# Attention and a routed feed-forward layer on one core: every engine's instruction order laid out anew, and six repeated products per batch removed

## The reference

```python
x = x + xattn(layernorm(x), ctx, ctx)      # x is (16, 128, 256), ctx (16, 128, 64)
x = x + ffn(layernorm(x), gate_w, w1, w2, w3)

# xattn: 32 query heads of 8 columns share 8 key/value heads
scores = einsum('bkgsd,bktd->bkgst', qh, kh) / sqrt(8)
out = einsum('bkgst,bktd->bkgsd', softmax(scores), vh)

# ffn: 8 experts, two chosen for each of the 2048 rows
probs = softmax(x @ gate_w.T)
weights, chosen = top_k(probs, 2);  weights = weights / weights.sum()
y = sum over the chosen e of weights[e] * (silu(x @ w1[e].T) * (x @ w3[e].T)) @ w2[e].T
```

## Time and profile before

| | |
|---|---|
| median of 3 runs | 457.79 us (457.29 to 458.43) |
| the profiled execution, its own time | 456.95 us |
| its span, first to last instruction | 455.1 us |
| busy: PE, DVE, ACT, POOL | 360.5, 236.6, 194.9, 196.3 us |
| mean granted TensorE clock | 0.933 of full speed |

### The profile page before, as it was taken

How to read it: one execution, slowest core, us unless ns; L and a number is a source line. 1 busy time by engine, 2 the same in 40 slices (tenths; PEclk the granted TensorE clock), 3 DMA queues, 4 the chain that set the end, 5 groups by cost and what they waited for, 6 DMA issues and landing times.

```text
span 455.1 us, 8617 instructions
## 1 busy us (share of the span) xinstructions
PE 360.5 (79%) x2255; PEld 256.4 (56%) x2256; DVE 236.6 (52%) x649; ACT 194.9 (43%) x397; POOL 196.3 (43%) x371
## 2 busy tenths in 40 slices
PE   0168789897988798752108999999999999999991
PEld 0044445454444354322107888888888888888871
DVE  6768777878777576638682322333222332223220
ACT  3325678675776465966303223222232222322220
POOL 6651355478564645575740223222233222332222
PEclk9999999999999898975557999999999999999997
DMA  6675877887988871320421332332333333223221
GB/s 191 163 146 108 254 217 217 202 237 192 256 230 246 200 219 65 120 81 23 163 81 35 49 59 46 49 56 46 58 47 47 56 47 58 46 47 57 36 23 23
DMA packets 46209, 51.16 MB, mean 112 GB/s; under 512 B 18659, under 2 KB 39267, under 8 KB 46179
## 3 DMA queue, kind: packets, MB, share of 16 engines
q1 hardware_dynamic: 37299, 39.64, 33.1%
q0 software_dynamic: 7152, 9.34, 13.1%
q10 hardware_dynamic: 1728, 1.82, 1.3%
HBM read 31.51 MB, written 16.69 MB: 106 GB/s over the span
## 4 chain that ended last, share of the span: by engine, by line
PE 53%; POOL 9%; issue 7%; DVE 5%; DMA 4%; ACT 3%; SPq 1%; POOLq 1%; ACTq 0%; DVEq 0%
PE bank L872 24%; PE bank L890 15%; PE bank L882 4%; DMA qst<-negT 3%; PE bank L704 2%; PE bank L860 2%; POOL slots_d L529 2%; PE bank L717 2%; PE bank L681 2%; ACT prob L941 1%; POOL x L500 1%; PE bank L678 1%; POOL rs L548 1%; DMA slots_d<-rows,slot 1%; DVE tx L1444 1%
## 5 line engine op out<-in xcount | busy, mean ns | idle before, releaser
L644 POOL DMA_INDIRECT out_rows<-ys,meta x39 | 60.6, 1554 | 153.0 <-DVE ys L1480 142.7
L1215 DVE TENSOR_REDUCE negm<-bank 128x4 f32<-128x512 f32 x128 | 83.2, 679 | 23.9 <-PE bank L681 23.3
L941 ACT ACTIVATE prob<-bank 128x512 f32<-128x512 f32 x128 | 73.6, 595 | 29.4 <-PE bank L704 28.0
L1473 DVE TENSOR_TENSOR gat<-bank,sil 128x512 f32<-128x512 f32 x39 | 27.0, 692 | 112.5 <-PE bank L872 112.5
L890 PE MATMUL bank<-w,gT 128*128 x312 | 73.9, 380 | 0.8 <-ACT gT L1135 0.8
L1129 ACT ACTIVATE sil<-bank 128x512 f32<-128x512 f32 x39 | 23.3, 597 | 105.9 <-PE bank L872 105.9
L704 PE MATMUL bank<-qst,kst 128*128 128x512 bf16 x128 | 49.6, 393 | 19.6 <-DMA qst<-negT 16.7
L872 PE MATMUL bank<-whi,xhi 128*128 x156 | 60.3, 468 | 1.2 <-ACT xhi L1123 1.2
L890 PEld LDWEIGHTS bank<-w,gT 128*128 128x128 f32 x312 | 56.3, 190 | 7.1 <-issue 1.0
L681 PEld LDWEIGHTS bank<-kst,qst 125*128 125x128 bf16 x512 | 41.4, 102 | 21.2 <-issue 3.1
L681 PE MATMUL bank<-kst,qst 125*128 125x128 bf16 x512 | 51.8, 227 | 0.0
(11 more groups left out here) (121 smaller groups left out, 493.7 us busy)
## 6 DMA issues: line engine op xcount, KB each, us to landing
xs<-slots_d SPq DMA_DIRECT2D x39, 129.0 KB, 2.1
w<-in_w1T SPq DMA_DIRECT2D x8, 512.0 KB, 4.6
w<-in_w3T SPq DMA_DIRECT2D x8, 512.0 KB, 4.6
w<-in_w2T SPq DMA_DIRECT2D x8, 512.0 KB
qparts_d<-qp SPq DMA_DIRECT2D x16, 192.0 KB, 5.4
qst<-qparts_d SPq DMA_DIRECT2D x16, 192.0 KB
qst<-qparts_d SPq DMA_DIRECT2D x16, 128.0 KB
vblk<-in_v SPq DMA_DIRECT2D x16, 128.0 KB
```

The lines of the kernel that those rows point to most:

```text
L644: pool.indirect_dma_start(out, IndirectOffsetOnAxis(ap=meta[:, r4, 0:1].bitcast(I32), axis=0), ys[:, r4, :], None, compute_op=ALU.add).the ...
L941: act.activation(prob[:, k, :], ps_e[k % 2][:, :], ACT.Exp, scale=SCALE).then_inc(exp_done, 1)
L1215: dve.tensor_reduce(negm[:, b % 2, g * G:(g + 1) * G], ps_s[(8 * b + g) % 3][:, :].rearrange("p (h t) -> p h t", h=G), AX.X, ALU.max, nega ...
L1473: dve.tensor_tensor(gat[:, u, :], ps_h3[u][:, :], sil, ALU.mult).then_inc(g_done, 1)
```

## The change

FILL becomes eight zeros, and the lists of all five engines are written in another order. The operations are the same otherwise, with one exception: ten of the eleven `split_lo` pieces that GpSimd had go to VectorE. Many operations now have one place in odd iterations and another in even ones. The numbers of iterations between a batch's steps remain, but a few steps move across an iteration's boundary. The core of the diff, with most of the moved calls left out:

```diff
-FILL = (1, 0, 1, 1, 1, 0, 1, 1)
+FILL = (0, 0, 0, 0, 0, 0, 0, 0)
...
             def store_k(j):
+                sp.wait_ge(k_split, (1, 3, 4)[j])
                 sp.dma_start(kparts_d[j], kp[:, j, :]).then_inc(kparts_out, 16)
...
             for i in range(-2, B):
-                if i == 7:
-                    load_w13(10)
-                if 3 <= i + 4 < B:
-                    write_q(i + 4)
-                if 2 <= i + 3 < B:
+                if i % 2 == 0 and 2 <= i + 3 < B:
                     stack_q(i + 3)
-                if 0 <= i + 1 < B:
+                if i % 2 == 0 and 0 <= i + 1 < B:
                     lay_neg(i + 1)
...
             for i in range(-2, B):
...
+                if i % 2 == 1 and 0 <= i + 1 < B:
+                    neg_split(i + 1, 3)
...
-            root_unit(7)
-            put_tokens(7)
-            split_lo(15)
+            add_res(15)
             add_seen(6)
-            add_res(15)
-            split_lo(17)
...
-            pe.wait_ge(lo_pool, 11)
-            pe.wait_ge(lo_late, N_SPLIT - 11)
+            pe.wait_ge(lo_pool, 1)
+            pe.wait_ge(lo_late, N_SPLIT - 1)
```

More of the change, by code:

```diff
@@ L345, in _ @@
             load_x(1)
+            load_x(3)
             load_x(2)
-            load_x(3)
+            load_x(8)
+            load_x(10)
+            store_k(0)
+            store_k(1)
             first_k(0)
[L349 to L352, removed]
             first_k(2)
             write_q(0)
-            store_k(1)
+            first_k(1)
             store_k(2)
-            load_x(10)
+            stack_q(0)
+            load_x(13)
+            write_q(1)
@@ new lines, in _ @@
+                if i % 2 == 1 and 0 <= i + 1 < B:
+                    lay_neg(i + 1)
+                if i == 7:
+                    load_w13(11)
+                if i % 2 == 1 and 3 <= i + 4 < B:
+                    write_q(i + 4)
+                if i % 2 == 0 and 3 <= i + 4 < B:
+                    write_q(i + 4)
+                if i == 11:
+                    load_w13(14)
+                if i == 5:
+                    load_w2(1)
+                if i == 4:
+                    load_w13(9)
@@ L425, in _ @@
[L425 to L432, removed]
+                if i == 12:
+                    load_w2(7)
+                if i % 2 == 0 and 2 <= i + 4 < B:
+                    load_k(i + 4)
+                if i == 8:
+                    load_w13(13)
@@ L579, in _ @@
             clear_q(3, 2)
-            clear_small()
             q_residual2(2)
             root_rows(2)
+            clear_small()
             for i in range(-2, B):
[L584 to L589, removed]
+                if i % 2 == 1 and 0 <= i + 1 < B:
+                    neg_split(i + 1, 3)
+                if i % 2 == 0 and 0 <= i + 1 < B:
+                    neg_split(i + 1, 3)
+                if i == 6:
+                    root_rows(4)
@@ L590, in _ @@
                 if i == 2:
                     root_rows(3)
+                if i % 2 == 1 and 0 <= i - 3 < B - 2:
+                    root_unit((i - 3) // 2)
                 if i == 6:
-                    root_rows(4)
-                if i == 6:
-                    split_lo(3)
+                    split_lo(2)
+                if i % 2 == 1 and 0 <= i - 5 < B - 2:
+                    scatter((i - 5) // 2, 0)
+                if i % 2 == 1 and 0 <= i - 1 < B:
+                    add_res(i - 1)
@@ L596, in _ @@
+                if i % 2 == 0 and 0 <= i - 1 < B:
+                    add_res(i - 1)
+                if i % 2 == 0 and 0 <= i - 4 < B - 2:
+                    add_seen((i - 4) // 2)
+                if i % 2 == 1 and 3 <= i + 5 < B:
+                    q_residual2(i + 5)
+                if i % 2 == 1 and 0 <= i - 5 < B - 2:
+                    scatter((i - 5) // 2, 1)
                 if i % 2 == 1 and 0 <= i - 3 < B - 2:
                     put_tokens((i - 3) // 2)
-                if i % 2 == 1 and 0 <= i - 3 < B - 2:
-                    root_unit((i - 3) // 2)
@@ L600, in _ @@
[L600 to L604, removed]
-                    q_residual2(i + 5)
[L606 to L610, removed]
+                if i % 2 == 0 and 3 <= i + 5 < B:
+                    q_residual2(i + 5)
@@ L620, in _ @@
-            root_unit(7)
-            put_tokens(7)
-            split_lo(15)
+                if i % 2 == 1 and 0 <= i + 2 < B:
+                    neg_split(i + 2, 1)
+                if i == 15:
+                    root_unit(7)
+                if i == 15:
+                    put_tokens(7)
+                if i % 2 == 0 and 0 <= i + 2 < B:
+                    neg_split(i + 2, 2)
+                if i % 2 == 1 and 0 <= i + 2 < B:
+                    neg_split(i + 2, 2)
+            add_res(15)
@@ L629, in _ @@
             put_tokens(8)
+            add_seen(7)
             scatter(7, 0)
[L631 to L633 removed]
             scatter(8, 0)
[L635 removed]
             pool.wait_ge(pads_out, 16 * (E + 2))
```

372 lines of the change are left out of this document (209 added, 163 removed).

## The result

| | kernel before | changed kernel |
|---|---|---|
| median, both in one session, 11 executions each | 458.43 us (455.1 to 461.89) | 454.22 us (450.72 to 456.24) |
| ratio, with its 95% interval | | 0.9925 (0.9896 to 0.9955) |
| the profiled execution, its span | 456.95, 455.1 us | 453.65, 451.7 us |
| mean granted TensorE clock | 0.933 | 0.905 |

The account below looks back on a forecast made before the run. In the loop TensorE was fullest, but waits on the maxima's transfer and GpSimd's chain counted. Loop 13 + tail 3.2 + head 2 = 18.2 us off 456.95 gave 438.7, stated as 438.5, range 426 to 453.

Parts of the forecast that it names:

- The loop: From batch 0's first e-product to batch 15's, 150.4 us before: 13 us gained, between 0 and 27.
- which adds no wait: SP's list keeps `stack_q` ahead of `lay_neg`, with `write_q` behind it; this was taken to cost no added wait.
- The pairs: Two batches with routing, from batch 5 on: 19.2 us in place of 20.9, five times 1.7, 8.5 us gained.
- The light batches: Batches 0 to 5 go at 8.3 us each in place of 9.2: 4.5 us gained, between 0 and 8.5.
- This covers most of the waits: Turning the maxima earlier in TensorE's list, by 1.1 to about 2 us, covers most waits in batches 0 to 4.
- GpSimd's odd iteration: In batches with routing, the maxima are split 14.5 us after the odd batch began; next odd batch after 19.2 us.
- The repeated products: Removing 96 idle repetitions, 21 us of TensorE's time in the loop, was counted at nothing by itself.
- The clock: Rival, chance 0.13: without repeated products, half clock at 13 more batch starts costs 20 us, giving 459, or 470 if longer.
- The wait only moves: Rival, chance 0.14: later `neg_split` eats the earlier turn's gain; pairs stay 20 to 21 us, 5 to 10 gained, 447 to 454.
- The tail: From batch 15's first e-product to the first expert tile: 1.3 + 3.0 - 1.1 = 3.2 us gained, between -1 and 5.
- Head and experts: Before batch 0's first e-product, `stack_q(1)` issued earlier gains 2 us, between 0 and 4; from first expert tile on, nothing.
- the lower bound of a pair: Two batches with the transfer at 5.2 us and GpSimd's root no earlier: taken as about 0 gained.

Follow-up runs that it names:

- e8_tail_pieces_on_dve: The kernel before with only the last four `split_lo` pieces moved from GpSimd's list to the end of VectorE's: 456.61 us, ratio 0.9893 (0.9848 to 0.9939).

## Why the prediction was wrong, step by step

**The loop, 13 us forecast: wrong.** It took 4.7 us more. The step that failed is the sentence that SP's list has `stack_q` ahead of `lay_neg` as before, "which adds no wait"; with it the transfer of the even batches' maxima got no term in the sum at all. The order of the two is as before, but in the new lists `lay_neg` follows close behind `stack_q`'s 384 KB, and the transfer then takes 6.8 us to land in place of the 4.0 that the even batches had before. In the odd batches, for which alone the 4.0 was put into the sum, it took 4.2. More readings would not have helped: all sixteen batches of the kernel before give 4.3 from issue to product.

*The pairs* from batch 5 on were forecast at 19.2 us each, from the odd batch's chain alone. They took 18.4, 21.9, 23.5, 24.6 and 18.4, together 106.8 us, where the forecast was 96 and the kernel before had 104.4. The two longest are those in which the even batch's maxima took longest, 8.8 us for batch 10 and 7.7 for batch 12. *The light batches*, from 0 to 5, took 48.4 us where 41.6 were forecast and 46.1 stood before. All six began as their maxima landed, in both kernels, and these took 5.7 us in the mean in place of 4.2. "This covers most of the waits" was therefore wrong: the earlier turn was met by a later landing.

The loops without the weights' traffic show that traffic is the rest of it: 11 us come back in the new order and none in the old. The prediction named this only in its last sentence, that the transfers' share of 0.75 rises over a shorter loop and that they could take longer than 5.2 us. It had neither a price nor a chance.

**GpSimd's odd iteration: right in size, but not what sets every pair.** The split ends 13.2 to 15.5 us after the odd batch's first e-product, 14.0 in the mean (forecast 14.5). In the pairs that end with batches 7, 9 and 15 the maxima are turned and `lay_neg` is issued within 0.6 to 0.7 us of that, as forecast, and the next odd batch starts 18.4, 21.9 and 18.4 us after the one before. In the pairs that end with batches 11 and 13 `lay_neg` follows the split only after 5.3 and 7.0 us. So the late split sets some pairs. What an earlier one would give was not tested, since the experiments left its last step behind the indirect transfers; TensorE's waits for it add to 4.4 us.

**The repeated products, nothing by themselves: right.** Three pairs of kernels with and without them lie within their intervals of each other, and a fourth has loops of 143.0 and 144.1 us.

**The clock: the rival's mechanism came, its price is not seen.** The loop spends 41 us at the lower level, 1.2 GHz, where it spent 7 before. That the stretch from 183 to 195 us spoke against a fall for this load was misread; it held for two batches. The Trainium skill ("TensorE: Matmul & The Clock Gate", What's actually happening) has the throttled clock as the default, which activity releases; the trace after agrees with 0.87 over its loop. But the repeated products were not what held it: with them in the new order it is 0.89. Nor is the rival's 20 us seen where the clock can be told apart. In the old order the loop has 31 us at half clock without the products and 7 with them, and the ratio is 0.9998; with the weights late it is 27 and 7, and the loops differ by 1.1 us, one profile each. In the changed kernel itself the cost stays open. From batch 10 on there are stretches in which TensorE is nearly full at half clock, and the first e-products of batches 11, 13, 14 and 15 start 0.9 to 2.2 us after their maxima have landed.

**"The wait only moves", 0.14: nearest, by another mechanism.** Its 447 to 454 hold the profiled execution's 453.65, and the median is at its edge. But it named the late split on GpSimd as what eats the gain, and kept the pairs at 20 to 21 us; the two longest pairs are those with the longest transfers of even batches. How much of the loss is the late split's, no run tells.

**The tail, 3.2 us forecast, 6.8 measured.** Mechanisms right, sizes off. The stall of the operation on 39 numbers gave its 3.0, and `e8_tail_pieces_on_dve` shows it alone. `add_res(15)` starts 16.5 us after batch 15's start (209.72) where it started 19.8 after (209.29), so 3.3 us in place of 1.3. The fourteen pieces took 8.52 us where 9.3 were forecast, 0.61 each in place of 0.66. That TensorE would wait for them was right.

**Head and experts.** 1.0 us in place of 2, inside its bounds, and 0.3 in place of 0.

**The sums.** Two do not come out as written. 438.7 us for the profiled execution, which is 0.8 under the median, gives 439.5 for the median and not 438.5. And the lower bound of a pair, the transfer at 5.2 and the root no earlier, is 1.7 - 1.2 - 1.3, a loss of 0.8 us a pair and 4 over the five, where "about 0 gained" was taken. With it the loop's range would have begun below zero, where the result fell.

**What stays open.** The stages add to the 3.4 us only with a loop of 4.7 us more, which is inside what single profiles scatter, as is the split of the gain between loop and tail. By the times, the four pieces of the tail alone are worth as much as all of the change, so the new order of the loop may have gained nothing. What holds the old order's loop at 151 us without the weights' traffic was not looked for. Whether the transfers' length comes of their bytes or of their number was not told apart: moving loads away took both. What an earlier split, or a full clock in the changed kernel's loop, would give is open, and so is why even doses of loads help.

## What to carry to other kernels

A transfer's length belongs to the order in which it was read. Before a list is moved, look at what will be issued just ahead of each small transfer on the chain, and price the two together: here the maxima took 2.8 to 3.0 us with nothing near, and 6.8 just behind 384 KB. Swapping them only moves the wait. Follow the chain of every iteration, not only of the one that looks fullest. Try loads that are due much later in even doses: it gave about 1% here, though by what is not shown. A half clock may cost nothing where the engine waits anyway, so compare kernels with and without the work that is meant to hold it before paying for that work. When an experiment moves an operation "behind" a chain of steps, look in its trace whether the last step ends earlier. And read TensorE's weight-load row beside its product row, since a missing product puts a wait under another line.

## What the runs showed of the hardware

- A transfer of 24 KB within the on-chip memory took 2.8 to 3.0 us from issue to landing where no `stack_q` had been issued in the 4 us before it, and 5.4 to 8.8 us where 384 KB had been issued on the same queue up to 0.6 us before it, in a loop with a DMA share of 0.74. Issuing the large loads from ScalarE's queue left the waits at 20.5 us. The Trainium skill ("DMA: Bandwidth & Descriptors", Issuing engines are not separate DMA queues) has it that transfers run on the same 16 DMA engines and interleave, whichever engine started them; the trace agrees as far as this goes.
- The granted clock was down for 31 us of a loop in which it had been down for 7, and the ratio of the times was 0.9998 (0.9959 to 1.0037).
- An operation of VectorE with two inputs from the on-chip memory took 3.18 us beside three GpSimd operations on 512 columns in a row, and ended 0.07 us after the last of them; it took 0.20 us without them, in two kernels. The Trainium skill ("SBUF — State Buffer", SBUF: two separate sides) describes the port pair that the two share as an exclusive lock, held for the whole instruction; the traces agree that VectorE was blocked, here by three instructions in a row.
